# Second attention: POOL compares the scores with the threshold and writes bfloat16 masks, DVE begins with the addition

## What is computed

```
dots = einsum('bhid,bhjd->bhij', q, k) * QK_SCALE
dots = einsum('hg,bgij->bhij', W_pre_th, dots)
dots = where(causal, mask_value, dots)
vk   = top_k(dots, 64)[0][..., -1:]
dots = where(dots < vk, mask_value, dots)
attn = softmax(dots)
attn = einsum('hg,bgij->bhij', W_post_th, attn)
out  = einsum('bhij,bhjd->bhid', attn, v)
```

## Time and profile before

| what | value |
|---|---|
| median of three runs | 3046.39 us |
| the profiled execution, its own time | 3044.7 us |
| its span, first to last instruction | 3042.6 us |
| mean granted clock of PE in it | 0.94 |
| busy in the span: PE, DVE, ACT, POOL | 2574.0, 2318.0, 2028.9, 1299.6 us |
| line 1402 (MAX8), 832 times | 368.5 us |
| line 1432 (attn), 480 of its instructions | 226.4 us |
| line 976 (wsc, on POOL), 512 times | 217.2 us |

### The profile page before, as it was taken

One profiled execution on the slowest core, in us unless ns is written; L12 is line 12 of the kernel. 1 busy time (PEld: TensorE's weight loads), 2 busy tenths in 40 slices (PEclk: granted clock), 3 DMA queues, 4 the chain that ended last, 5 costly groups with the idle time before them and its releaser, 6 DMA issues. The chain is left out here.

```text
span 3042.6 us, 58896 instructions
## 1 busy us (share of the span) xinstructions
PE 2574.0 (85%) x18372; PEld 1572.8 (52%) x18372; DVE 2318.0 (76%) x7745; ACT 2028.9 (67%) x5415; POOL 1299.6 (43%) x3717
## 2 busy tenths in 40 slices
PE   4699999998888888888888888888888888776998
PEld 1233444434345565565565565565555565555565
DVE  4656666664339989989889898998998997995654
ACT  1366655665358878878878878887887887773331
POOL 2212222211016656656655655655655665673000
PEclk6799999999969999999999999999999998996999
DMA  2111111101011121212212112112112112121532
GB/s 103 44 32 39 43 44 40 32 17 52 11 43 36 40 47 40 43 37 44 44 27 57 42 22 63 38 28 57 41 32 56 32 37 53 29 45 42 120 90 59
DMA packets 111291, 137.00 MB, mean 45 GB/s; under 512 B 20448, under 2 KB 90592, under 8 KB 110464
## 3 DMA queue, kind: packets, MB, share of 16 engines
q1 hardware_dynamic: 109968, 132.00, 18.0%
q10 hardware_dynamic: 1008, 1.18, 0.1%
HBM read 47.56 MB, written 13.24 MB: 20 GB/s over the span
## 5 line engine op out<-in xcount | busy, mean ns | idle before, releaser
L1280 ACT ACTIVATE junk<-xs,thr 128x420 bf16<-128x420 f32 (+12 forms) x832 | 465.7, 569 | 72.7 <-POOL thr L995 57.7
L1121 PE MATMUL pt<-wsc,attn 128*128 128x128 f32 x2560 | 361.6, 290 | 101.2 <-POOL wsc L976 64.3
L1108 PE MATMUL pm<-mixin,pre_b 128*128 128x258 f32 (+15 forms) x1088 | 367.4, 453 | 92.2 <-ACT xs L1273 80.3
L1121 PEld LDWEIGHTS pt<-wsc,attn 128*128 128x128 f32 x2560 | 323.7, 199 | 191.3 <-POOL wsc L976 132.2
L1402 DVE MAX8 best<-left 128x8 f32<-128x420 f32 (+12 forms) x832 | 368.5, 483 | 0.0
L1074 PE MATMUL pa<-kT,qT 64*128 64x258 f32 (+3 forms) x1280 | 291.3, 455 | 83.4 <-ACT arena L1242 59.3
L1242 ACT ACTIVATE arena<-pa,nrm 128x258 f32<-128x258 f32 (+3 forms) x640 | 274.1, 478 | 102.8 <-PE pa L1074 95.7
L1432 DVE SCALAR_TENSOR_TENSOR attn<-xs,bound,ex 128x420 f32<-128x420 f32 (+14 forms) x480 | 226.4, 500 | 119.0 <-issue 57.8
L1108 PEld LDWEIGHTS pm<-mixin,pre_b 128*128 128x128 f32 x1088 | 177.0, 200 | 228.2 <-issue 195.4
L1299 ACT COPY at<-pt 128x128 f32<-128x128 f32 (+3 forms) x512 | 198.2, 450 | 110.5 <-PE po L1159 93.0
L1289 ACT ACTIVATE ex<-xs,negm 128x228 f32<-128x228 f32 (+15 forms) x512 | 239.3, 519 | 0.1
(11 more groups left out here) (261 smaller groups left out, 5849.0 us busy)
## 6 DMA issues: line engine op xcount, KB each, us to landing
spread<-gates_dram SPq DMA_DIRECT2D x32, 512.0 KB, 7.8
mixin<-arena SPq DMA_DIRECT2D x32, 258.0 KB
mixin<-arena SPq DMA_DIRECT2D x32, 242.0 KB
mixin<-arena SPq DMA_DIRECT2D x32, 226.0 KB
mixin<-arena SPq DMA_DIRECT2D x32, 210.0 KB
mixin<-arena SPq DMA_DIRECT2D x32, 194.0 KB
q_stack<-parts_dram SPq DMA_DIRECT2D x96, 64.0 KB
parts_dram<-parts SPq DMA_DIRECT2D x15, 384.0 KB, 2.3
```

The costliest lines, as they stand in the source:

```text
L1108: ins = nc.tensor.matmul(bank[:, 0:jn], pre_b[:, :], mixin[:, m % MIX_SLOTS, j0:j0 + jn], start=True, stop=not last)
L1121: ins = nc.tensor.matmul(bank[:, P * k:P * k + P], attn[:, m % A_SLOTS, P * k:P * k + P], wsc[:, m % A_SLOTS], start=True, stop=True)
L1280: ins = nc.scalar.activation(junk[:, z, 0:width(n)], xs[:, m % X_SLOTS, 0:width(n)], ACT.Sign, scale=-1.0, bias=thr[:, s % LIVE, z:z + 1], ...
```

## The change

The comparison of the scores with the threshold moves from DVE to POOL (function `taken_off`). It writes a new tile `over`, with room for one pair of units, in bfloat16. POOL issues it as the last thing of its turn on thresholds, after the second correction, and waits for its own correction (`thr_done[1]`) and until DVE has read the pair before (`over_read`). DVE waits for `over_done` in place of `thr_done[1]` and begins with the addition, which now reads `over` and `xs` and writes `left`; its completion is told by `over_read`, for which the first MAX8 waits as well.

```diff
--- before.py
+++ after.py
@@ -763,6 +763,7 @@
         ex = sb("ex", [P, E1_SLOTS, J])
         junk = sb("junk", [P, PAIR, J], BF16)
         left = sb("left", [P, PAIR, J])
+        over = sb("over", [P, PAIR, J], BF16)
         attn = sb("attn", [P, A_SLOTS, J])
         wsc = sb("wsc", [P, A_SLOTS, P])
         top = sb("top", [P, PAIR, 8])
@@ -797,6 +798,7 @@
         negm_done, moments_done = sem("negm_done"), sem("moments_done")
         thr_ready = sem("thr_ready")
         thr_done, counted = ([sem(f"{n}{r}") for r in range(COUNTS)] for n in ("thr_done", "counted"))
+        over_done, over_read = sem("over_done"), sem("over_read")
         ex_done, summed, attn_done = sem("ex_done"), sem("summed"), sem("attn_done")
         ssq_done, rooted = sem("ssq_done"), sem("rooted")
         var_done, rstd_done, x3_done = sem("var2_done"), sem("rstd2_done"), sem("x3_done")
@@ -994,6 +996,17 @@
                     chain.link(nc.gpsimd.tensor_tensor(shift[:, p], shift[:, p], slopes[:, p], ALU.mult))
                     nc.gpsimd.tensor_tensor(thr[:, p], thr[:, p], shift[:, p], ALU.add).then_inc(thr_done[r], 1)
 
+                def taken_off(s):
+
+                    q, p = search_nth[s] - 1, s % LIVE
+                    pool.wait_ge(thr_done[-1], q + 1)
+                    if q:
+                        pool.wait_ge(over_read, PAIR * q)
+                    for z, m, n in pair_of(s):
+                        ins = nc.gpsimd.tensor_scalar(over[:, z, 0:span(s)], xs[:, m % X_SLOTS, 0:span(s)], thr[:, p, z:z + 1], TAKEN,
+                                                      ALU.is_gt, ALU.mult)
+                    ins.then_inc(over_done, 1)
+
                 def inverse_root(b, o):
 
                     pool.wait_ge(var_done, TT * b + o + 1)
@@ -1010,6 +1023,8 @@
                     for r in range(1, COUNTS):
                         if s - 1 in search_nth:
                             corrected(s - 1, r)
+                    if s - 1 in search_nth:
+                        taken_off(s - 1)
                     for what in beside.get(s - 1, []):
                         if what[0] == "wo":
                             inverse_root(*what[1:])
@@ -1384,21 +1399,19 @@
 
                 def near_threshold(s):
 
-                    wn, p = span(s), s % LIVE
-                    dve.wait_ge(thr_done[-1], search_nth[s])
+                    wn = span(s)
+                    dve.wait_ge(over_done, search_nth[s])
                     done = [None] * PAIR
                     taken = [above[:, m // SUBS % 2, n:n + 1] for z, m, n in pair_of(s)]
                     for z, m, n in pair_of(s):
-                        done[z] = chain.mark(nc.vector.tensor_scalar(left[:, z, 0:wn], xs[:, m % X_SLOTS, 0:wn], thr[:, p, z:z + 1], TAKEN,
-                                                                     ALU.is_gt, ALU.mult))
-                    for z, m, n in pair_of(s):
-                        chain.after(done[z])
-                        done[z] = chain.mark(nc.vector.scalar_tensor_tensor(out=left[:, z, 0:wn], in0=left[:, z, 0:wn], scalar=1.0,
-                                                                            in1=xs[:, m % X_SLOTS, 0:wn], op0=ALU.mult, op1=ALU.add,
-                                                                            accum_out=taken[z]))
+                        nc.vector.scalar_tensor_tensor(out=left[:, z, 0:wn], in0=over[:, z, 0:wn], scalar=1.0, in1=xs[:, m % X_SLOTS, 0:wn],
+                                                       op0=ALU.mult, op1=ALU.add, accum_out=taken[z]).then_inc(over_read, 1)
                     for k in range(WINDOW // 8):
                         for z in range(PAIR):
-                            chain.after(done[z])
+                            if k:
+                                chain.after(done[z])
+                            else:
+                                dve.wait_ge(over_read, PAIR * (search_nth[s] - 1) + z + 1)
                             done[z] = chain.mark(nc.vector.max(out=best[:, z, 8 * k:8 * k + 8], in_=left[:, z, 0:wn]))
                         if k < WINDOW // 8 - 1:
                             for z in range(PAIR):
```

## The result

The changed kernel took 3245.45 us (median of four runs, 3243.43 to 3251.57), the kernel before 3047.83 beside it (3036.9 to 3056.61). The ratio is 1.0636, with a 95% interval of 1.0598 to 1.0673. Forecast were 3000 us and a range from 2955 to 3065. The sign was wrong, and the loss of 198 us is more than four times that of the slower rival (3092 us, a loss of 46).

What follows compares the result with a forecast made beforehand. DVE alone was taken to set the pace for about two thirds of a batch, sharing it with PE for a fifth. Terms -86 + 26 + 10 + 4 = -46, called -45, on 3044.7 us gave 3000 us; range 2955 to 3065.

Steps and rivals of the forecast that it cites:

- slower rival: POOL would hold up DVE's `picked`, `attn` and next additions longer than the comparison cost: +47 us, 3092 us; chance 0.16.
- The price on POOL: POOL's comparison was put at 1.1 ns per column, 0.55 us each, 1.1 us a pair.
- The relief of DVE: Of 124 us taken off DVE, 10.8 per batch would shorten the kernel, 86 us in eight batches.
- the exclusion: POOL's comparison would block DVE's additions, `picked` or `attn` in every second step: 26 us, bounds 10 and 125.
- lateness: POOL's scaling behind the comparison would come 0.7 us late in a third of steps: 10 us, bounds 0 and 49.
- DVE's waits: DVE would wait some 0.5 us for POOL's mask at the first narrow step, once or twice per batch: 4 us.
- the rival of the hidden gain: PE and ACT set the pace, or DVE waits longer for exponentials; only wide steps gain: 3037 us; chance 0.21.
- the comparison above 0.8 us: Sign of a wrong forecast: POOL's new operation takes more than 0.8 us, where 0.55 on average was expected.
- DVE's additions waiting for `over`: Sign of a wrong forecast: DVE's additions wait for POOL's mask; near no idle time was expected except at narrow steps.
- PE's wait for `wsc` doubled: Sign of a wrong forecast: PE's wait for POOL's `wsc`, 61.1 us before the change, doubles.
- DVE's idle time up by as much as its work went down: Sign of a wrong forecast: DVE's idle time grows by the work removed, expected at about 140 us.

Runs made afterwards that it cites:

- p1: Changed kernel plus 48 POOL instructions after its end, timed alone at 132 and 512 columns: is_gt·mult 3.30 ns per column, mult·mult 0.83.
- e5: Changed kernel with mult·mult in place of is_gt·mult on POOL over all columns, missed-row test off: 3050.37 us, ratio 1.0007 to the kernel before.
- e1: Changed kernel with no comparison on POOL or DVE, `over` zero throughout, missed-row test off: 3017.76 us, ratio 0.9912 to the kernel before.
- e6: e1 with both of ACT's counts over only a quarter of the columns: 2942.57 us, ratio 0.9638 to the kernel before.
- e8: Kernel before with both of ACT's counts over only a quarter of the columns, missed-row test off: 3030.23 us, ratio 0.9923.
- e2: Changed kernel with POOL comparing only the first quarter of the columns, missed-row test off: 3048.55 us, ratio 0.9993 to the kernel before.
- e3: Changed kernel, but DVE also compares for itself and waits only for the threshold; POOL's result is unread: 3257.83 us, ratio 1.0686.
- e11: e3 with POOL's unread comparison moved behind the scaling of the next turn, reading weights in place of scores: 3359.49 us, ratio 1.1034.
- e12: Changed kernel with POOL's two powers per step replaced by multiplications, missed-row test off: 3151.43 us, ratio 1.0349 to the kernel before.
- e10: Changed kernel with POOL comparing both units by add·mult into uint8, DVE multiplying while it adds: 3084.93 us, ratio 1.0102.
- e9: Changed kernel with POOL comparing only the second unit, by add·mult into uint8; DVE compares the first as before: 3071.58 us, ratio 1.0053.

## Why the prediction was wrong

By its own terms, in the order of the sum:

- **The price on POOL**, "I take 1.1 ns, between these two", with ends of 0.91 and 1.6 us: the step that failed. It is 3.3 ns per column, 2.8 us per step on average, outside both ends. The failing idea was that the nearest row is the one with the same instruction name. Line 976 is TENSOR_SCALAR with a scalar per row and two steps, but its steps are mult and mult, a pair that is nearly four times as quick per column (p1). The trace had no row with a comparison on POOL, and an upper end from a TENSOR_TENSOR was no bound. Even for line 976 the slope was misread: 1.42 ns per column came from rows of 2 and 128 columns, and p1 has 0.83 between 132 and 512. By e5, which has about the price I took, and the changed kernel, this error is 195 us of the 245 by which the forecast missed.
- **The relief of DVE**, "I count all 6.05" in the wide steps and half of the rest: 86 us forecast, 27 measured (e1). The work went as said, 122 us in all (2318.0 to 2196.1) and 5.9 us in eight wide steps, but of the latter 3.0 came through, and the rest of the fifth batch gave nothing more (batch 237.6 us before, 236.5 in e1). "98.7% busy" was read as "alone sets the pace". e6 and e8 show the other engine of the loop: ACT's counts, whose relief is worth as little alone and more than twice as much together with DVE's.
- **The costs beside it**, 26 for the exclusion, 10 for lateness, 4 for DVE's waits: 40 in sum, against 25 to 29 at the forecast price (e1 to e2 and e5). That the sum came near is luck, since the split did not hold. The hold-ups were there (37 us in e5, and 14 us in the changed kernel, by the same two groups: 237.8 and 81.0), but 30 us more or less of them ended at the same time. What is left is lateness of POOL; that is concluded by exclusion, and PE's clock (below) may have a part in it.
- **DVE waits for the mask**, 4 us: 6.5 at the forecast price (e5), 113.9 at the true one, and even those explain little of the loss (e3).
- **The rivals.** With the right relief the same sum, -27 and +28, gives no change: that is the rival of the hidden gain (3037 us, 3031 to 3061 as same), and e2 and e5 bear it out at that price. The slower rival had the right sign by the wrong mechanism: it expected POOL to exclude DVE, for 0.92 us per step. The loss came from POOL's program order, in which `wsc` and the next threshold stand behind the comparison (e3, e11, e12). I had that mechanism among the terms, with 0 to 49 us as bounds, made from the wrong price. The sentence of the Trainium skill that I set beside this rival (GPSIMD Engine Reference, Engine selection: elementwise work on a tile belongs on VectorE) held here for the comparison, at 386 ns on average on DVE (line 1392 before) against 1412 on POOL. What it grants one-input operations, nearly the full rate, can hold at most for the three quick pairs and the cast, at 0.83 and 0.84 ns per column, and not for the comparison at 3.3 or mult alone at 2.5.
- **The signs named in advance** did tell: "the comparison above 0.8 us", "DVE's additions waiting for `over`", "PE's wait for `wsc` doubled" (61.1 to 198.5) and DVE's idle time up by as much as its work went down (by 295 us, against 96) all came. The fifth batch took 263.6 us, where 232 were forecast.

Open is the share of PE's clock. Its mean granted clock fell from 0.94 to 0.904, and its busy time rose from 2574.0 to 2667.4 us with the same 18372 instructions. The matmuls of line 1136 last 272 to 582 ns with a median of 275 in both kernels, but their mean rose from 290 to 310, which fits a larger share of them at the lower clock. The slowest kernels have the lowest granted clock (e3 0.899, e11 0.884), but e1, faster than the kernel before, has 0.933. No run separated how much of the 198 us the clock adds. Nor does any run say why mult alone is slower than mult·mult.

## What to carry to other kernels

Before work moves to another engine, find a row with the same operations on that engine, not only the same instruction name. If there is none, measure it by itself or leave the upper end open: here one probe of 50 us would have shown the price. An engine that is 98% busy can still be one of two that take turns, so count its relief in full only if the others' waits show that they stand still for it. Free time on a serving engine is worth what its next customers let it be: look at what stands behind the new work in its program order.

## What was unexpected of the hardware

- On POOL, TENSOR_SCALAR with mult·mult, add·mult or mult·add took 1.48 us per pair at 512 columns. Every other pair tried, with is_gt, max, min or subtract in it or add·add, took 3.9 to 4.1, one operation alone 3.2, and a TENSOR_TENSOR subtraction 2.6. The output's type (float32, bfloat16, uint8) made no difference.
- How much POOL held DVE up did not follow POOL's busy time: against e1, 584 us of is_gt·mult lengthened `attn` and `picked` by 14 us, in e5 250 us of mult·mult by 37, and in e10 244 us of add·mult by 11 (237.5 and 78.2). Which instructions meet differs between these kernels, and no run separates that from the operation.
- Converting a large float32 to uint8 on POOL gave 255 and a negative one 0 (e9 and e10, which count with 255), so that a quick pair, 0.59 us on average in e10, can serve as a comparison.
